# The projection's bias: a product on TensorE, or a value that ScalarE writes into the bank beforehand

## What is computed

```
qkv  = (x @ w_qkv) split into q, k, v and 8 heads of 64     # x: 16 x 1024 x 512, fp32
attn = softmax(where(adj == 0, -inf, q k^T / 8))            # 1024 x 1024 for each batch and head
o    = (attn v) @ w_proj + b_proj
ln   = (o - mean(o)) * rsqrt(var(o) + 1e-5) * gamma + beta
out  = layernorm(x + o + ln)
```

## Time and profile before

| | |
|---|---|
| Profiled execution, own time | 3239.09 us |
| Its span | 3237.3 us |
| Median of the runs | 3241.94 us |
| PE busy | 3056.4 us, 94% |
| POOL busy | 2719.2 us, 84% |
| ACT busy | 2553.9 us, 79% |
| DVE busy | 2265.5 us, 70% |
| Transposing DMA queue | 91.7% of 16 engines' span |
| Granted PE clock, mean | 0.98 |

### The profile page before, as it was taken

One profiled execution on the slowest core, in us unless ns is written; L12 is line 12 of the kernel. 1 busy time (PEld: TensorE's weight loads), 2 busy tenths in 40 slices (PEclk: granted clock), 3 DMA queues, 4 the chain that ended last, 5 costly groups with the idle time before them and its releaser, 6 DMA issues.

```text
span 3237.3 us, 120659 instructions
## 1 busy us (share of the span) xinstructions
PE 3056.4 (94%) x42624; PEld 1909.3 (59%) x42624; DVE 2265.5 (70%) x4371; ACT 2553.9 (79%) x3723; POOL 2719.2 (84%) x1543
## 2 busy tenths in 40 slices
PE   6989999999999999999999999999999999999984
PEld 3555656656666656656656656656656566656652
DVE  5556777676776767767777776767767777777764
ACT  5887888788887878878787887878878788888870
POOL 3668989798998979979898997979979898898994
PEclk9999999999999999999999999999999999999997
DMA  7999999999999999999999999999999999999992
GB/s 205 193 178 195 214 191 221 185 217 200 206 219 185 218 190 213 217 187 216 189 215 206 204 215 185 218 193 212 218 181 216 195 215 206 199 218 191 217 203 71
DMA packets 2187660, 648.94 MB, mean 200 GB/s; under 512 B 2135379, under 2 KB 2135379, under 8 KB 2187605
## 3 DMA queue, kind: packets, MB, share of 16 engines
q1 hardware_dynamic: 2133604, 548.02, 91.7%
q10 hardware_dynamic: 54000, 100.16, 9.6%
HBM read 77.60 MB, written 33.55 MB: 34 GB/s over the span
## 4 chain that ended last, share of the span: by engine, by line
POOL 60%; issue 29%; PE 3%; SPq 2%; DMA 2%; DVE 1%; ACT 1%; POOLq 1%; ACTq 0%; DVEq 0%
POOL p_split L718 49%; POOL x_res L737 4%; POOL x_res L728 4%; SPq L278 2%; POOL norm L734 2%; POOL norm L731 2%; DMA pt<-p_split 2%; PE proj L365 1%; PE side L347 1%; PE scores_a L383 1%; POOLq L717 0%; ACT p L475 0%; PE side L336 0%; ACT p_split L488 0%; DMA x_in<-in_x 0%
## 5 line engine op out<-in xcount | busy, mean ns | idle before, releaser
L718 POOL TENSOR_TENSOR p_split<-p,p_split 128x1024 f16<-128x1024 f32 x1024 | 2172.0, 2139 | 453.6 <-ACT p_split L488 451.7
L475 ACT ACTIVATE p<-p,row_min 128x1024 f32<-128x1024 f32 x1024 | 1168.2, 1142 | 128.8 <-DVE row_min L612 124.7
L488 ACT ACTIVATE p_split<-p 128x1024 f16<-128x1024 f32 x1024 | 1052.2, 1048 | 215.3 <-DMA pt<-p_split 212.3
L612 DVE CUSTOM_DVE_ANT_0 p<-scores_a,mask_q 128x1024 f32<-128x1024 f32 x512 | 625.8, 1222 | 469.1 <-PE scores_b L383 449.7
L404 PE MATMUL pv_bank<-v_both,pt 128*128 128x64 f16 x8192 | 834.1, 194 | 21.7 <-DMA pt<-p_split 19.7
L405 PE MATMUL pv_bank<-v_both,pt 128*128 128x64 f16 x8192 | 834.6, 194 | 0.0
L406 PE MATMUL pv_bank<-v_both,pt 128*128 128x64 f16 x8192 | 834.6, 194 | 0.0
L404 PEld LDWEIGHTS pv_bank<-v_both,pt 128*128 128x128 f16 x8192 | 744.0, 99 | 117.1 <-issue 34.7
L405 PEld LDWEIGHTS pv_bank<-v_both,pt 128*128 128x128 f16 x8192 | 733.1, 99 | 83.2 <-issue 4.4
L406 PEld LDWEIGHTS pv_bank<-v_both,pt 128*128 128x128 f16 x8192 | 733.6, 99 | 0.0
L612 DVE CUSTOM_DVE_ANT_0 p<-scores_b,mask_q 128x1024 f32<-128x1024 f32 x512 | 624.2, 1219 | 4.0 <-POOL p_split L718 0.9
(11 more groups left out here) (68 smaller groups left out, 5079.7 us busy)
## 6 DMA issues: line engine op xcount, KB each, us to landing
x_res<-in_x ACTq DMA_DIRECT2D x128, 256.0 KB, 3.4
out<-x_res ACTq DMA_DIRECT2D x128, 256.0 KB, 3.4
x_in<-in_x ACTq DMA_DIRECT2D x63, 512.0 KB, 4.6
pt<-p_split SPq DMA_TRANSPOSE x1024, 4.8
pt<-in_adj SPq DMA_DIRECT2D x8, 512.0 KB, 9.7
ot<-in_L_gnn_w_qkv SPq DMA_DIRECT2D x4, 768.0 KB, 8.8
x_in<-in_x SPq DMA_DIRECT2D x4, 512.0 KB, 7.5
ot<-in_L_gnn_w_proj SPq DMA_DIRECT2D x4, 256.0 KB, 7.1
```

Source lines behind the costliest of these rows:

```text
L475: nc.scalar.activation(p32[:, slot, :], p32[:, slot, :], ACT.Exp, bias=row_min[:, slot:slot + 1], scale=-1.0, accum_out=row_sum[:, head:he ...
L488: nc.scalar.activation(p_split[:, head % RING, HI, :], p32[:, head % RING, :], ACT.Copy).then_inc(hi_done, 1)
L612: nc.vector.tensor_tensor_reduce(out=p32[:, slot, :], in0=scores[ab][:, :], in1=mask_q[:, u, :], scale=-SCALE, scalar=3.0e38, op0=ALU.add, ...
L718: nc.gpsimd.tensor_tensor(p_split[:, slot, LO, :], p32[:, slot, :], p_split[:, slot, HI, :], ALU.subtract).then_inc(lo_done, 1)
```

## The change

The 13th product of each projected tile is taken out. In its place ACT writes the bias, times 256 as the products are, into the whole bank before the tile's first product, and none of the 12 products starts the bank afresh, so that all 12 add to what stands there. For this the bias is loaded once to all partitions (256 KB), and at the kernel's start PE makes four products of the identity into `proj`, which mark the bank's elements as written. ACT does this at slot 9 for P0 and at slot 26 for P1, after `summed`, and raises `seeded`, for which PE now waits in place of `summed`. The copies that made `bias_rows` go. The projection's lengths in `ORDER` and `LENGTH` go from 13 to 12, and so the items move among the slots.

```diff
-         13), ("XT", 1, 2), ... ("P1", 0, 13),
+ ORDER = [... ("P0", 4, 9), ("XT", 0, 1), ("P0", 9, 12), ("XT", 1, 2), ... ("P1", 0, 12),
+ SEED_SLOT = [9, 26]
-        ones = sb("ones", [P, P], F16)
-        bias_rows = sb("bias_rows", [P, D], F16)
+        bias_b = sb("bias_b", [P, D], F32)
-            for row in (0, BIAS_LO):
-                sp.dma_start(x_res[row:row + 1, 0, :], b_proj...).then_inc(const_loaded, 16)
+            for dst, src in ((gamma_b, gamma), (beta_b, beta), (bias_b, b_proj)):
@@ tensor
+            for k in range(KC):
+                mm = nc.tensor.matmul(proj[:, k * P:(k + 1) * P], ident[:, :], ident[:, :], start=(k == 0), stop=True,
+                                      skip_group_check=True)
+            mm.then_inc(bits_set, 1)
-                    wait_alone(pe, summed, projected(g, half))
+                    wait_alone(pe, seeded, projected(g, half) + 1)
-                                          (wp_hi, wp_hi, wp_lo)[part][:, k, :], start=(i == 0), stop=False)
-                else:
-                    nc.tensor.matmul(proj[:, :], ones[:, :], bias_rows[:, :], start=False, stop=True).then_inc(proj_ready, 1)
+                                      (wp_hi, wp_hi, wp_lo)[part][:, k, :], start=False, stop=(i == 3 * KC - 1),
+                                      skip_group_check=True)
+                if i == 3 * KC - 1:
+                    mm.then_inc(proj_ready, 1)
@@ scalar
+            def seed(n):
+                if known(n) and n == 0:
+                    act.wait_ge(const_loaded, 48)
+                    act.wait_ge(bits_set, 1)
+                wait_alone(act, summed, n)
+                nc.scalar.activation(proj[:, :], bias_b[:, :], ACT.Copy, scale=WSCALE).then_inc(seeded, 1)
...
+                    if s == SEED_SLOT[0] and active(g, "P0"):
+                        seed(projected(g, 0))
+                    if s == SEED_SLOT[1] and active(g, "P1"):
+                        seed(projected(g, 1))
                     if s == 1:
                         load_next(g)
```

More of the change, by code:

```diff
@@ L28 @@
 EPS = 1e-5
-BIAS_LO = 32
-ORDER = [("Q1", 0, 12), ("V0", 0, 48), ("V1", 0, 48), ("P0", 0, 4), ("O1", 0, 4), ("P0", 4, 9), ("XT", 0, 1), ("P0", 9,
-         13), ("XT", 1, 2), ("XT", 2, 3), ("XT", 3, 4), ("Q0", 0, 12), ("K0", 0, 12), ("K1", 0, 12), ("P1", 0, 13),
+ORDER = [("Q1", 0, 12), ("V0", 0, 48), ("V1", 0, 48), ("P0", 0, 4), ("O1", 0, 4), ("P0", 4, 9), ("XT", 0, 1), ("P0", 9, 12), ("XT", 1, 2), ("XT", 2, 3), ("XT", 3, 4), ("Q0", 0, 12), ("K0", 0, 12), ("K1", 0, 12), ("P1", 0, 12),
          ("O0", 0, 4)]
@@ L41 @@
 NEXT_READY = [kind for kind in SIDE if kind in ("Q0", "K0", "K1")][-1]
-LENGTH = {"Q1": 12, "V0": 48, "V1": 48, "O1": 4, "Q0": 12, "K0": 12, "K1": 12, "O0": 4, "P0": 13, "P1": 13, "XT": 4}
+LENGTH = {"Q1": 12, "V0": 48, "V1": 48, "O1": 4, "Q0": 12, "K0": 12, "K1": 12, "O0": 4, "P0": 12, "P1": 12, "XT": 4}
 COST = {"Q": 9, "V": 2.5, "O": 5, "K": 9, "P": 9, "X": 0}
@@ L206, in attention_block @@
         ident_zero, ident_ready, half_set = sem("ident_zero"), sem("ident_ready"), sem("half_set")
-        bias_ready, bias_zero = sem("bias_ready"), sem("bias_zero")
+        bits_set, seeded = sem("bits_set"), sem("seeded")
         w_hi_ready, w_ready, mask_ready = sem("w_hi_ready"), sem("w_ready"), sem("mask_ready")
@@ L266, in _ @@
                 sp.dma_start(wp_in[:, kc, :], w_proj[kc * P:(kc + 1) * P, :]).then_inc(wp_loaded, 16)
-            for dst, src in ((gamma_b, gamma), (beta_b, beta)):
+            for dst, src in ((gamma_b, gamma), (beta_b, beta), (bias_b, b_proj)):
                 sp.dma_start(dst[:, :], src.rearrange("(o n) -> o n", o=1).broadcast_to([P, D])).then_inc(const_loaded, 16)
-            for row in (0, BIAS_LO):
-                sp.dma_start(x_res[row:row + 1, 0, :], b_proj.rearrange("(o n) -> o n", o=1)).then_inc(const_loaded, 16)
             sp.wait_ge(mask_ready, T)
@@ L356, in project @@
                         pe.wait_ge(w_ready, 4 * KC)
-                        pe.wait_ge(bias_ready, 4)
-                    wait_alone(pe, summed, projected(g, half))
+                    wait_alone(pe, seeded, projected(g, half) + 1)
                     if half == 0:
@@ L362, in project @@
                         wait_alone(pe, side_dve, side_done(g, "O1") if active(g, "O1") else side_before(g))
-                if i < 3 * KC:
-                    k, part = i // 3, i % 3
-                    mm = nc.tensor.matmul(proj[:, :], ot[:, (HI, LO, HI)[part], parity(c), k, t, :],
-                                          (wp_hi, wp_hi, wp_lo)[part][:, k, :], start=(i == 0), stop=False)
-                else:
-                    nc.tensor.matmul(proj[:, :], ones[:, :], bias_rows[:, :], start=False, stop=True).then_inc(proj_ready, 1)
+                k, part = i // 3, i % 3
+                mm = nc.tensor.matmul(proj[:, :], ot[:, (HI, LO, HI)[part], parity(c), k, t, :],
+                                      (wp_hi, wp_hi, wp_lo)[part][:, k, :], start=False, stop=(i == 3 * KC - 1),
+                                      skip_group_check=True)
+                if i == 3 * KC - 1:
+                    mm.then_inc(proj_ready, 1)
             def unit_scores(g, u):
@@ L498, in load_residual @@
                     return
-                if known(g) and g == PAIRS:
-                    act.wait_ge(bias_ready, 4)
                 wait_alone(act, stored[i], (g - PAIRS) * 16)
@@ L545, in _ @@
         def _(dve):
-            nc.vector.memset(bias_rows[:, :], 0.0).then_inc(bias_zero, 1)
-            nc.vector.memset(ones[:, :], 1.0).then_inc(bias_ready, 1)
             def prepare_weights():
@@ L565, in prepare_projection @@
                                                    ALU.mult, ALU.subtract).then_inc(w_ready, 2)
[L566 to L569, removed]
             def transposed(g, i):
@@ L706, in _ @@
             pool.wait_ge(half_set, 1)
-            pool.wait_ge(const_loaded, 64)
+            pool.wait_ge(const_loaded, 48)
             def low_part(g, u, ab):
@@ L714, in low_part @@
                 slot = (2 * uk + ab) % RING
-                if known(ug) and ug == 0 and uk == 0 and ab == 0:
-                    pool.wait_ge(bias_ready, 4)
                 pool.wait_ge(hi_done, heads(ug, uk, ab) + 1)
```

## The result

The changed kernel took 3258.51 us, the median of six runs (3253.41 to 3262.91), against 3241.95 us for six of before: a ratio of 1.0053, 95% interval 1.0042 to 1.0063. It is slower by 0.5%, 16.6 us. The profiled execution took 3257.16 us, its span 3255.3.

What follows compares the result with a forecast made beforehand. PE sets the main stage's pace; DVE's sum holds each end-stage tile. Terms -10 (60 groups), +1.5 (x transposes), -0.7 (start), +4.5 (end) sum to -4.7, say -4 us: 3238 us by the runs' median, range 3223 to 3257.

Steps and rivals of the forecast that it cites:

- rival 2: Slot 13: the whole 0.79 us delay reaches the landing, V product waits in every group; +16 us, 3258 us; chance 0.25.
- The product taken away: Groups 4 to 63: two bias products of 0.22 us go and items spread anew; 0.37 us saved in a group.
- The seed's price: ACT: each seed takes 0.57 us, bounds 0.4 and 0.75; two in a group are 1.1 us.
- The seed at slot 26: ACT, between exponentials of pieces 12 and 13: POOL's work moves 0.79 us against the next group; 0.4 reaches piece 15's landing.
- The seed at slot 9: ACT, before an exponential: 0.97 us late, 0.81 covered; PE stalls 0.2 us a group before the first V product, slot 13.
- The groups with x transposes: 15 groups: ACT gets the second tile later; +0.1 us each, 1.5 us in all, bounds -0.2 and +0.6 each.
- Start and end: Start gains 0.7 us; in the end stage the seed is on the path, +4.5 us, bounds +2 and +9.
- a change above 0.6 us against the others: Groups with x transposes: changing by more than 0.6 us against the other groups would show the forecast wrong.

Runs made afterwards that it cites:

- the kernel with the copy: Kernel before, its 13 products kept, plus one idle 128x512 ACT copy, SBUF to SBUF, at slot 26: 3242.22 us, ratio 1.0004.
- no bias: Changed kernel without seeds, 12 products, the first starting the bank, b_proj left out of the result: 3199.22 us, ratio 0.9868 against before.
- the seed at 28: Changed kernel with seeds at slots 9 and 28, P1's first two products moved from slot 27 to 28: 3263.67 us, ratio 1.0067 against before.

## Why the prediction was wrong

The forecast was 3238 us and a range from 3223 to 3257; the time is 3258.5, the size that rival 2 gave (3258). That agreement is luck in good part: rival 2 had +11 us from a stall at V's take, while the sum below has +22 from a stall at Q's take and a gain of 10 that it didn't have. By its steps:

**The product taken away: right.** 0.37 us in a group forecast, 0.41 found without any bias. Units 2 and 6 became shorter by 0.22 us each there (forecast 0.1 and 0.2), and unit 7 longer by 0.10.

**The seed's price: right.** The changed kernel's rows of the seed:

```profile
L440 ACT ACTIVATE proj<-bias_b 128x512 f32<-128x512 f32 x128 | 74.6, 583 | 61.8 <-DVE x_res L658 61.8
```

583 ns, and 0.52 us from its start to the next instruction's (1493.84 to 1494.36), against 0.57. The idle copy of the same shape into SBUF took 615 ns in its run. The Trainium skill's sentence in "ScalarE: Activation LUTs", section "Step-by-step: what each stage is for", that PSUM is the lower-latency destination for an ACTIVATE, agrees in sign; here it is 5%.

**The seed at slot 26: this step failed.** Its first half held. POOL is late, and against the group's start the issue of piece 13 is late by 0.62 us in the mean (0.79 forecast). The second half was: "The load of x, 512 KB, is issued in the same microseconds and is not moved. So part of the delay goes into DMA time that is busy anyway." For piece 15, which I followed, that held: its issue is late by 0.74 us, its landing by 0.60 (13.71 to 14.31; 0.4 forecast). For piece 13 the reverse happened. Its transposition slipped from 0.50 us ahead of the load to 0.18 us behind it, and 0.94 us came on top of the delay: it landed 1.56 us late, and PE waited 39.3 us in the run for the take of Q that stands behind it. The forecast worked out the delay of one landing, piece 15's, and left out piece 13's, for which Q's take waits. It took one moving term against a fixed one without asking which of the two would then come first. Both times stand in the same stretch of the trace, 0.5 us apart, and the delay that I had worked out was larger than that.

**The seed at slot 9: its cost was right, the place of the stall wrong.** Alone it costs 3 us in the run. The cover ahead of V's take held (35.1 us of idle time down to 12.5). PE's wait at V's take grew by 3.7 us in the run, 0.06 in a group, where I had 0.2. The stall came one take earlier, at Q's, where I had worked out no cover. It is there that piece 13 lands at 8.50 us without harm in the kernel with the copy, and at 9.47 with harm in the change. Mean lengths of the units in the 43 groups, from scores to scores (us):

```
kernel      0     1     2     3     4     5     6     7    group
before    5.92  5.55  5.70  5.77  5.72  5.74  5.93  5.81   46.14
no bias   5.90  5.50  5.48  5.78  5.72  5.74  5.71  5.91   45.73
changed   5.85  6.32  5.48  5.78  5.74  5.73  5.77  5.95   46.62
```

Unit 1, with Q's take, is 0.77 us longer than before and 0.82 longer than without a seed; in it PE's recorded wait for `q_lo` is 0.65 us a group, and 0.02 in the two others. The waits for row minima also grew against before, from 18.0 to 26.4 us in the run, but they are 25.0 without a seed and so belong to the 0.41. Rival 2 named the wait for Q's take in half a sentence; its working rested on V's take.

**The groups with x transposes: the clock was left out.** By the forecast such a group changes by -0.17 + 0.1 = -0.07 us; in the mean of 14 it changed by -0.69 (56.33 to 55.64). Of these groups 12 had a stretch with TensorE at the lower of its clock levels before, and 5 after. At the full clock they hardly differ: 54.69 us in the mean of 2 before, 54.76 of 9 after, and 53.99 of 7 without bias. So the gain of 10 us is that fewer groups were slowed, and not a cheaper group. Group 31 is such a pair, with a granted clock of 0.97 and 1.00 above. The prediction named a change above 0.6 us against the others here as a sign that it is wrong; it is 1.2.

**Start and end.** The start gained: group 4 begins 2.6 us earlier, where I had counted 0.7. The end stage grew by 7.0 us in place of 4.5, inside the bounds. Its rounds answer to the earlier trace rows:

```profile
3192.78 1.01 PE L364 MATMUL proj<-wp_hi,ot 128*128 128x512 f16 x2 [4.48 <-ACT proj L440]
...
3202.43 1.01 PE L364 MATMUL proj<-wp_hi,ot 128*128 128x512 f16 x2 [4.47 <-ACT proj L440]
```

The wait is 0.70 us longer than 3.78, as worked out (0.73). What is left over the forecast fits the clock, for which, with the residual's load, I had allowed 1.5 us: the granted mean of this stage fell from 0.80 to 0.69. In this round every pair of products lasts 1.01 to 1.06 us, in a full-clock round of before 0.59.

The sum of the spans: 45 ordinary groups x 0.48 = +22, 14 groups x -0.69 = -10, the start -3, the last group +2, the end +7: +18 us, 3237.3 to 3255.3.

**What stays open.** Why piece 13 takes 0.9 us more with the load 0.2 us ahead, and nothing more with it 0.6 or 1.3 us ahead, isn't known. The order doesn't settle it: in the kernel with the copy 18 groups have the load ahead by 0.12 us in the mean and no loss, and with the seed at 28 piece 13 goes first by 0.89 us and takes 7.14. Shown is that the late landing makes the stall, and that at the late issue a smaller or an earlier load takes both away. Nor did any run show why the groups with x transposes fall to the lower clock more often in one kernel than in another.

## What to carry to other kernels

When an edit delays the issue of a DMA, list what other queues issue within that delay, and ask which comes first afterwards. Here a transfer that was issued 0.62 us later, behind the load and not ahead of it, landed 1.56 us later. Order alone didn't tell the price here, so measure the landing of every piece near the place, and not only of the one at the end of the chain. And cost each use of a shared pair of banks by its own cover: the stall appears at the first one that has none.

## What the runs showed of the hardware

From issue to landing, with what is still left of the piece before it, the transposition of piece 13 took 4.30 us in the mean with the 512 KB load issued 5.2 us behind it, 4.87 and 5.59 with it 1.6 and 1.5 us behind, 6.0 with it 0.3 to 0.5 us behind, 6.9 with it 0.2 us ahead, 5.6 with it 0.6 or 1.3 us ahead, and 4.8 with 256 KB 0.2 us ahead. Two kernels don't fit a rule of the lead alone: 7.14 with the load 0.89 us behind (seed at 28), and 5.98 in 18 groups with it 0.12 us ahead (the copy). A group with x transposes takes 54.7 us in the kernel before and in the changed one at the full clock, and 55.9 to 58.5 us with a stretch at the lower level; which it is differs from group to group of one execution. Writing 128x512 fp32 from SBUF took ACT 583 ns into PSUM and 615 ns into SBUF.
